# Who multiplies the high one-hots: ScalarE or GpSimd, in the routing stage of an attention and expert kernel

## The chip, the cores and the metric

The kernel runs on one core of one Trainium2 chip. The metric is the device time of one execution in microseconds (us). A core has five engines that run side by side and wait for one another by semaphores: TensorE (PE in the profile; its weight loads are PEld), VectorE (DVE), ScalarE (ACT), GpSimd (POOL) and SyncE (SP), which issues transfers.

## The reference, cut to what matters

The input x has 4096 rows of 256 numbers. It goes through a layer norm and cross attention, then through a layer norm and a block of 8 experts, of which each row takes two. The part that this case is about decides where each row goes:

```python
scores = softmax(x @ wg)                      # [4096, 8]
gates, idx = top_k(scores, 2)                 # two experts for each row
masks = one_hot(idx, 8)                       # [4096, 2, 8]
loc = cumsum(masks, 0) - 1 + offsets          # place in the expert's list
keep = loc_sel < C                            # C = 1280 places each
pos = where(keep, idx * C + loc_sel, E * C)
buf.at[pos].set(x)                            # rows sorted by expert
y = silu(disp @ fc1 + b1) @ fc2 + b2          # per expert
combined = sum(gates * ybuf[pos])             # back to the rows
```

The kernel needs the inverse of `pos`: for each of the 8 x 1280 = 10240 places, the number of the row that stands there. With that it gathers the rows of 256 places at a time.

## The kernel before, in words

**Stages.** For 32 tiles of 128 rows the attention runs until about 279 us of the profiled span. Then comes routing, the stage of this case. From about 309 us to 727 us the experts run: 40 steps of 256 places, each with transposes, a first and a second product on TensorE. A last stage adds and normalizes.

**The inverse table.** Each row's two choices give 64 columns of 128 choices (NC = 64, one per partition and column). A place number is split into `slot_hi` (which group of 128 places, 80 of them, NS = 80) and `slot_lo` (which of the 128). For each column two one-hot matrices are made:

- the low one, `oh_lo[:, n, :]`, 128 wide in bf16. Where the low number fits it holds the number of the row's tile plus one, elsewhere zero. VectorE makes it in one instruction a column (`lo_chunk`, L1478). ScalarE makes it in two (`lo_onehot`): a square of the difference into `apart` (L788), then a Relu that keeps what is zero (L793).
- the high one, `oh_id[:, ring, column, 1, :]`, 80 wide in bf16, made for a whole chunk of columns in one VectorE instruction (`hi_chunk`, L1474). A copy multiplied by the number of the partition, `oh_id[..., 0, :]`, stands beside it (`rows_of_chunk`, L802, on ScalarE before).

TensorE then multiplies: one matmul a column, 64 in all, added up in bank 2 (L1155, `placed` counts them). The half from `oh_id[..., 0, :]` gives row number times tile number, the half from `oh_id[..., 1, :]` gives the tile number. VectorE turns both into `slot_ids` (`rows_ids`, L1637 to L1651) and GpSimd gathers by them (L599).

**The order.** The code's order on each engine is the order in which it runs; nothing schedules it. The 64 columns are cut into chunks, and TensorE takes the chunks in the order of the table:

```python
CHUNKS = [(0, 7), (7, 14), (14, 21), (28, 37), (37, 46), (21, 28), (46, 55), (55, 64)]
BY_ACT = (0, 1, 2, 5)
RING = 5
```

Columns 0 to 27 (the early part) have their places before the last tiles are done. Columns 28 to 63 have theirs when VectorE has signalled `located` (after L1451). `BY_ACT` names the chunks whose low one-hots ScalarE makes; VectorE makes the others. `oh_id` is a ring of five chunks, so the sixth waits until TensorE has placed the first, and so on.

Beside this GpSimd makes the gates (L622 to L632). Behind its last product of the gates it waits for `ids_made` and starts the gathers. Behind its last low one-hot VectorE makes one low part of weights (`first_weights_lo(0)`, L1458), then waits for all 64 matmuls. Behind its last product ScalarE makes two high parts of weights (L729) and loads a table.

Of the kernel before, what the change touches and what calls it, by code (L numbers as in the profile page):

```python
# [5 lines left out]
def xattn_moe_kernel(nc, x, ctxT, wqT, bq, wkT, bk, wvT, bv, woT, wo, bo, boT, wg, w1T, b1T, w2, b2, gamma, beta, out):  # L6
# [13 lines left out]
    f32, f32r, bf16, i32 = mybir.dt.float32, mybir.dt.float32r, mybir.dt.bfloat16, mybir.dt.int32  # L20
    ALU, ACT, AX = mybir.AluOpType, mybir.ActivationFunctionType, mybir.AxisListType.X
    ds = bass.ds

    P = 128
# [38 lines left out]
    def wait(engine, sem, value):  # L63

        if not isinstance(value, int) or value > 0:
            engine.wait_ge(sem, value)
# [16 lines left out]
    with root:  # L83
        def sb(name, shape, dt=f32, where=root):
            return where.enter_context(nc.sbuf_tensor(name, shape, dt))
# [88 lines left out]
        hi_i = sb("hi_i", [P, NC], i32, A)  # L174
        slot_hi = sb("slot_hi", [P, NC], f32, A)
        slot_lo = sb("slot_lo", [P, NC], f32, A)
        CHUNKS = [(0, 7), (7, 14), (14, 21), (28, 37), (37, 46), (21, 28), (46, 55), (55, 64)]
        BY_ACT = (0, 1, 2, 5)
        RING = 5
        oh_lo = sb("oh_lo", [P, NC, P], bf16, A)  # L180
        oh_id = sb("oh_id", [P, RING, 9, 2, NS], bf16, A)
        apart = sb("apart", [P, 2, 7, P], bf16, A)
        sid = sb("sid", [P, NS], f32, A)
        tile_1 = sb("tile_1", [P, NS], f32, A)
# [66 lines left out]
        def sem(name):  # L251
            return sems[name]
# [71 lines left out]
        def columns_before(k):  # L324
            return sum(b - a for a, b in CHUNKS[:k])

# [112 lines left out]
        def _(pool):  # L439
# [163 lines left out]
            def scatter(st):  # L603

                if within(st, NST):
# [3 lines left out]
                    for q in range(2):  # L609
# [2 lines left out]
                                             y_sb[:, u, q, :], None, bounds_check=N + 4 * P - 1, oob_is_err=False,  # L612
                                             compute_op=ALU.add).then_inc(scattered[u], 16)

            pool.wait_ge(load_b1, 16)
            g.tensor_copy(b1_now[:, 0, :], b1_sb[:, 0:HJ]).then_inc(sem("b1_copied"), 1)

# [4 lines left out]
            g.tensor_tensor(e_all[:], below[:], rstd2[:].unsqueeze(2).to_broadcast([P, NT, NE]), ALU.mult)\  # L622
                .then_inc(sem("router_scaled"), 1)
            g.tensor_tensor(e_second[:], second[:], rstd2[:], ALU.mult).then_inc(sem("router_scaled"), 1)
            pool.wait_ge(sem("located"), 1)
            g.tensor_tensor(either[:], sel[:, 0], sel[:, 1], ALU.add).then_inc(sem("gate_parts"), 1)
            pool.wait_ge(sem("router_exp"), 2)
# [3 lines left out]
            pool.wait_ge(sem("gate_parts"), 2)  # L631
            g.tensor_tensor(gate_e[:], either[:], e_scale[:].unsqueeze(2).to_broadcast([P, NT, NE]), ALU.mult)\  # L632
                .then_inc(sem("gates_made"), 1)

            for u in range(2):
                pool.wait_ge(xn_stored[u], 32 * PAIRS)
# [30 lines left out]
        def _(act):  # L667
# [114 lines left out]
            def lo_onehot(k):  # L782

                a0, b0 = CHUNKS[k]
                i = BY_ACT.index(k)
                wait(act, sem("lo_made_act"), i - 1)
                for n in range(a0, b0):
                    m = a.activation(apart[:, i % 2, n - a0, :], iota_lo[:], ACT.Square, scale=-1.0,  # L788
                                     bias=slot_lo[:, n:n + 1])
                m.then_inc(sem("lo_apart"), 1)  # L790
                act.wait_ge(sem("lo_apart"), i + 1)
                for n in range(a0, b0):
                    m = a.activation(oh_lo[:, n, :], apart[:, i % 2, n - a0, :], ACT.Relu, scale=-float(n + 1),  # L793
                                     bias=tile_no[:, n:n + 1])
                m.then_inc(sem("lo_made_act"), 1)

            def rows_of_chunk(k):
                a0, b0 = CHUNKS[k]
                act.wait_ge(sem("hi_made"), k + 1)
                wait(act, sem("placed"), columns_before(k - RING + 1) if k >= RING else 0)  # L800
                o = oh_id[:, k % RING, 0:b0 - a0]
                a.activation(o[:, :, 0, :], o[:, :, 1, :], ACT.Copy, scale=my_row[:, 0:1]).then_inc(sem("row_made"), 1)  # L802

            act.wait_ge(sem("route_consts"), 10)
            act.wait_ge(sem("early_located"), 1)
# [2 lines left out]
            act.wait_ge(sem("router_scaled"), 2)  # L808
            a.activation(e_all[:], e_all[:], ACT.Exp).then_inc(sem("router_exp"), 1)
            a.activation(e_second[:], e_second[:], ACT.Exp).then_inc(sem("router_exp"), 1)  # L810
            rows_of_chunk(0)
            rows_of_chunk(1)
            lo_onehot(2)
            for k in (2, 3, 4):
                rows_of_chunk(k)
            lo_onehot(5)
            for k in range(5, len(CHUNKS)):
                rows_of_chunk(k)

            def rows_hi(gq, c):  # L820
                if within_st(gq, c):
# [439 lines left out]
        def _(dve):  # L1261
# [193 lines left out]
            def first_weights_lo(n):  # L1455
                dve.wait_ge(sem("w_hi_made"), n + 1)
                hi, lo, raw = w_parts(0, n)
                v.tensor_tensor(lo, raw, hi.bitcast(f32), ALU.subtract).then_inc(sem("w_lo_made"), 1)  # L1458
# [11 lines left out]
            def hi_chunk(k):  # L1470

                wait(dve, sem("placed"), columns_before(k - RING + 1) if k >= RING else 0)
                o, iota, at = hi_onehot(k)
                v.tensor_tensor(o, iota, at, ALU.is_equal).then_inc(sem("hi_made"), 1)  # L1474

            def lo_chunk(k):
                for n in range(*CHUNKS[k]):
                    m = v.tensor_scalar(oh_lo[:, n, :], iota_lo[:], slot_lo[:, n:n + 1], float(n % NT + 1),  # L1478
                                        ALU.is_equal, ALU.mult)
                m.then_inc(sem("lo_made"), 1)  # L1480
# [142 lines left out]
            lo_chunk(4)  # L1623
            hi_chunk(5)
            hi_chunk(6)
            lo_chunk(6)
            hi_chunk(7)
            lo_chunk(7)
            first_weights_lo(0)

            dve.wait_ge(sem("placed"), NC)
# [154 lines left out]
```

## Time and profile before

| what | value |
|---|---|
| median of 3 runs | 775.68 us (772.46 to 775.83) |
| the profiled execution, its own time | 773.96 us |
| its span in the trace | 772.2 us |
| busy over the span | PE 679.7 us, DVE 564.8, POOL 431.6, ACT 408.5 |
| routing, first low one-hot on ACT to last matmul of the table | 272.47 to 299.16 us |

The trace gives for each instruction its start from the span's beginning and its duration. Instructions that stand in one engine's queue without a wait overlap a little, so a duration can be longer than the distance from one start to the next; where an engine works through a row of them, the distance is what counts. Spans on POOL are rough.

### The profile page before, as it was taken

Reading aid. Unit: us, or ns where it says so; the run is one execution under the profiler, and the core shown is the slowest. Engines: PE = TensorE matmul, PEld = TensorE weight load, DVE = VectorE, ACT = ScalarE, POOL = GpSimd, SP = SyncE. Lnnn points to the kernel's source line nnn. Section 1 sums busy time; section 2 is a strip of 40 time slices with the busy share of each in tenths; the row PEclk is TensorE's granted clock in tenths of the full one; section 3 lists DMA queues with packets and bytes.
Section 4 is the critical chain, followed back from the end, with each engine's and each line's share of the span. In section 5 each row is a group of like instructions: output and inputs, shape, how many; then the busy total and the mean of one; then the engine's idle time right before and its main releaser. Section 6 shows DMA issues by size and latency. Waiting matters only on the chain.

```text
span 772.2 us, 15699 instructions
## 1 busy us (share of the span) xinstructions
PE 679.7 (88%) x5592; PEld 647.8 (84%) x5592; DVE 564.8 (73%) x1194; ACT 408.5 (53%) x963; POOL 431.6 (56%) x547
## 2 busy tenths in 40 slices
PE   5999999999999823999999999999999999999600
PEld 4789898888989723999999998999999999999500
DVE  5589898988887896666566669777596665854187
ACT  3445555555555585444544557455474454643185
POOL 6745565466465333535455558857577454632456
PEclk9789999999999955999999999999999999999855
DMA  9501011010110121533343456544455243322484
GB/s 295 173 15 42 30 41 41 31 42 29 42 40 31 42 84 39 174 81 55 88 105 45 101 111 119 118 81 94 102 116 115 46 103 57 58 28 29 55 273 149
DMA packets 55764, 64.10 MB, mean 83 GB/s; under 512 B 9472, under 2 KB 50944, under 8 KB 55552
## 3 DMA queue, kind: packets, MB, share of 16 engines
q0 software_dynamic: 15360, 21.31, 17.3%
q1 hardware_dynamic: 39616, 41.64, 16.5%
q8 instruction: 55, 0.90, 0.5%
q14 instruction: 29, 0.24, 0.1%
q10 hardware_dynamic: 704, 0.01, 0.0%
HBM read 39.22 MB, written 23.72 MB: 82 GB/s over the span
## 4 chain that ended last, share of the span: by engine, by line
PE 70%; DVE 19%; issue 4%; POOL 2%; ACT 2%; DMA 2%; POOLq 0%; SPq 0%; DVEq 0%; ACTq 0%
PE banks L898 18%; PE banks L900 17%; PE banks L899 17%; PE banks L1040 5%; PE banks L1026 3%; PE banks L1170 2%; DVE rowmax L1497 2%; PE banks L1014 2%; DVE vals L1465 2%; DVE xn1T_lo L1294 1%; DVE st L1271 1%; PE banks L1069 1%; DVE probs L1504 1%; PE banks L943 1%; DVE X L1556 1%
## 5 line engine op out<-in xcount | busy, mean ns | idle before, releaser
L611 POOL DMA_INDIRECT sum_rows<-y_sb,slot_ids x80 | 133.2, 1665 | 160.3 <-ACT y_sb L841 143.9
L851 ACT ACTIVATE hraw<-banks,b_now 128x256 f32<-128x256 f32 x320 | 132.3, 476 | 88.9 <-PE banks L900 81.5
L898 PE MATMUL banks<-xT_hi,w_hi 128*128 128x256 f32 x560 | 161.6, 289 | 1.7 <-ACT xT_hi L823 1.7
L900 PE MATMUL banks<-xT_hi,w_lo 128*128 128x256 f32 x560 | 158.5, 283 | 0.0
L899 PE MATMUL banks<-xT_lo,w_hi 128*128 128x256 f32 x560 | 158.4, 283 | 0.0
L898 PE MATMUL banks<-w_hi,h_hi 128*128 128x256 f32 x528 | 148.8, 282 | 1.3 <-issue 1.3
L899 PE MATMUL banks<-w_lo,h_hi 128*128 128x256 f32 x528 | 148.6, 281 | 0.0
L900 PE MATMUL banks<-w_hi,h_lo 128*128 128x256 f32 x528 | 148.5, 281 | 0.0
L1689 DVE TENSOR_TENSOR h_lo<-hraw,h_hi 128x512 fp32r<-128x512 f32 x160 | 113.8, 711 | 5.5
L1687 DVE CAST h_hi<-hraw 128x512 fp32r<-128x512 f32 x160 | 79.0, 494 | 44.8 <-ACT hraw L851 43.7
L898 PEld LDWEIGHTS banks<-xT_hi,w_hi 128*128 128x128 f32 x560 | 106.4, 190 | 2.2 <-issue 2.1
L599 POOL DMA_INDIRECT xg<-xn_rows,slot_ids x80 | 89.1, 1113 | 32.9 <-issue 32.3
L899 PEld LDWEIGHTS banks<-xT_lo,w_hi 128*128 128x128 f32 x560 | 106.5, 190 | 0.1
L900 PEld LDWEIGHTS banks<-xT_hi,w_lo 128*128 128x128 f32 x560 | 106.3, 190 | 0.0
L898 PEld LDWEIGHTS banks<-w_hi,h_hi 128*128 128x128 f32 x528 | 99.4, 188 | 1.7 <-issue 1.7
L738 ACT ACTIVATE probsT<-banks 124x384 f32<-124x384 f32 (+1 forms) x128 | 56.0, 437 | 84.5 <-PE banks L1026 84.3
L899 PEld LDWEIGHTS banks<-w_lo,h_hi 128*128 128x128 f32 x528 | 99.4, 188 | 0.0
L900 PEld LDWEIGHTS banks<-w_hi,h_lo 128*128 128x128 f32 x528 | 99.4, 188 | 0.0
L823 ACT ACTIVATE xT_hi<-banks 128x512 fp32r<-128x512 f32 x40 | 24.1, 602 | 115.2 <-PE banks L1170 107.2
L1040 PE MATMUL banks<-VB,probsT 124*128 124x51 f32 (+2 forms) x640 | 83.0, 268 | 0.0
L1040 PEld LDWEIGHTS banks<-VB,probsT 124*128 124x128 f32 x640 | 81.6, 192 | 0.0
L574 POOL TENSOR_TENSOR rstd<-var,minus_half 128x1 f32<-128x1 f32 x32 | 17.5, 547 | 98.3 <-DVE var L1575 98.3
(216 smaller groups left out, 1442.6 us busy)
## 6 DMA issues: line engine op xcount, KB each, us to landing
w1raw<-in_w1T SPq DMA_DIRECT2D x8, 1024.0 KB
w2raw<-in_w SPq DMA_DIRECT2D x8, 1024.0 KB
xn_rows<-xn SPq DMA_DIRECT2D x32, 128.0 KB, 1.8
sum_rows<-xn SPq DMA_DIRECT2D x32, 128.0 KB, 1.8
out<-z SPq DMA_DIRECT2D x16, 256.0 KB, 2.2
res<-sum_rows SPq DMA_DIRECT2D x7, 512.0 KB, 8.4
X<-in_x SPq DMA_DIRECT2D x2, 1280.0 KB, 12.4
xg<-xn_rows,slot_ids POOLq DMA_INDIRECT x80
```

The source lines that it names most:

```text
L599: g.indirect_dma_start(xg[:, st % XR, q, :], None, xn_rows, bass.IndirectOffsetOnAxis(ap=slot_ids[:, st, 0, q:q + 1], axis=0), bounds_chec ...
L611: g.indirect_dma_start(sum_rows, bass.IndirectOffsetOnAxis(ap=slot_ids[:, st, 1, q:q + 1], axis=0), y_sb[:, u, q, :], None, bounds_check=N ...
L738: a.activation(probsT[:, j0:j0 + w, :].rearrange("r j q -> r (j q)"), banks[0:JW, PT, 0:w * P], ACT.Copy).then_inc(sem("pT_made"), 1)
L823: a.activation(xT_hi[:, c % 2].rearrange("p c t -> p (c t)"), banks[:, XT, :], ACT.Copy)\
L851: a.activation(hraw[:, j // 2, j % 2, :], banks[:, j // 2, (j % 2) * 256:(j % 2 + 1) * 256], ACT.Silu, bias=b1_now[:, (c // SPE) % 2, j:j ...
L898: t_.matmul(o, a_hi, b_hi, start=first, stop=False)
L899: t_.matmul(o, a_hi, b_lo, start=False, stop=False)
L900: return t_.matmul(o, a_lo, b_hi, start=False, stop=last)
L1026: m = t_.transpose(banks[0:JW, PT, (j - j0) * P:(j - j0 + 1) * P], probs[:, 1 - u, f * KH + j * JS:f * KH + j * JS + JW], ident[:])
L1040: m = t_.matmul(banks[:, PV, f * VW + a_:f * VW + a_ + n_], probsT[:, NJ * f + j, :], VB[:, ds(((2 * b + f) * NJ + j) * VW + a_, n_)], sta ...
L1687: v.tensor_copy(hi, raw).then_inc(sem("h_hi_made"), 1)
L1689: v.tensor_tensor(lo, raw, hi.bitcast(f32), ALU.subtract).then_inc(sem("h_lo_made"), 1)
```

## The change

The multiplication of the high one-hots by the row number goes from ScalarE's `activation` with a scale to GpSimd's `tensor_scalar`. ScalarE gets one more chunk of low one-hots (chunk 6). There are nine chunks in place of eight: 7, 7, 7, 8, 8, 7, 7, 7 and 6 columns, where before there were four of 7 and four of 9. The ring's entries are 8 columns wide instead of 9. Since ScalarE now makes low one-hots for columns past 32 as well, its tile numbers are taken modulo NT = 32.

```diff
-        CHUNKS = [(0, 7), (7, 14), (14, 21), (28, 37), (37, 46), (21, 28), (46, 55), (55, 64)]
-        BY_ACT = (0, 1, 2, 5)
+        CHUNKS = [(0, 7), (7, 14), (14, 21), (28, 36), (36, 44), (21, 28), (44, 51), (51, 58), (58, 64)]
+        BY_ACT = (0, 1, 2, 5, 6)
         RING = 5
         oh_lo = sb("oh_lo", [P, NC, P], bf16, A)
-        oh_id = sb("oh_id", [P, RING, 9, 2, NS], bf16, A)
+        oh_id = sb("oh_id", [P, RING, 8, 2, NS], bf16, A)
...
+            def rows_of_chunk(k):
+                a0, b0 = CHUNKS[k]
+                pool.wait_ge(sem("hi_made"), k + 1)
+                wait(pool, sem("placed"), columns_before(k - RING + 1) if k >= RING else 0)
+                o = oh_id[:, k % RING, 0:b0 - a0]
+                g.tensor_scalar(o[:, :, 0, :], o[:, :, 1, :], my_row[:, 0:1], None, ALU.mult)\
+                    .then_inc(sem("row_made"), 1)
...
             g.tensor_tensor(e_second[:], second[:], rstd2[:], ALU.mult).then_inc(sem("router_scaled"), 1)
+            rows_of_chunk(0)
+            rows_of_chunk(1)
             pool.wait_ge(sem("located"), 1)
...
                 .then_inc(sem("gates_made"), 1)
+            for k in range(2, len(CHUNKS)):
+                rows_of_chunk(k)
...
-            def rows_of_chunk(k):
-                a0, b0 = CHUNKS[k]
-                act.wait_ge(sem("hi_made"), k + 1)
-                wait(act, sem("placed"), columns_before(k - RING + 1) if k >= RING else 0)
-                o = oh_id[:, k % RING, 0:b0 - a0]
-                a.activation(o[:, :, 0, :], o[:, :, 1, :], ACT.Copy, scale=my_row[:, 0:1]).then_inc(sem("row_made"), 1)
...
-            rows_of_chunk(0)
-            rows_of_chunk(1)
             lo_onehot(2)
-            for k in (2, 3, 4):
-                rows_of_chunk(k)
             lo_onehot(5)
-            for k in range(5, len(CHUNKS)):
-                rows_of_chunk(k)
+            act.wait_ge(sem("located"), 1)
+            lo_onehot(6)
...
             hi_chunk(6)
-            lo_chunk(6)
             hi_chunk(7)
             lo_chunk(7)
+            hi_chunk(8)
+            lo_chunk(8)
             first_weights_lo(0)
```

ScalarE's queue from the second exponential of the gates to the end of the table's work, before (`oh_id` with `my_row` is the multiplication, `apart` and `oh_lo` are the two halves of the low one-hots):

```order
L810 ACTIVATE e_second<-e_second 128x32
L802 ACTIVATE oh_id<-oh_id,my_row 128x7x80 [waits hi_made] x2
L788 ACTIVATE apart<-iota_lo,slot_lo 128x128 [waits lo_made_act]
L788 ACTIVATE apart<-iota_lo,slot_lo 128x128 x6
L793 ACTIVATE oh_lo<-apart,tile_no 128x128 [waits lo_apart]
L793 ACTIVATE oh_lo<-apart,tile_no 128x128 x6
L802 ACTIVATE oh_id<-oh_id,my_row 128x7x80 [waits hi_made]
L802 ACTIVATE oh_id<-oh_id,my_row 128x9x80 [waits hi_made] x2
```

and the last of it, in the changed kernel:

```order
L805 ACTIVATE oh_lo<-apart,tile_no 128x128 x6
L800 ACTIVATE apart<-iota_lo,slot_lo 128x128 [waits lo_made_act,located]
L800 ACTIVATE apart<-iota_lo,slot_lo 128x128 x6
L805 ACTIVATE oh_lo<-apart,tile_no 128x128 [waits lo_apart]
L805 ACTIVATE oh_lo<-apart,tile_no 128x128 x6
L741 ACTIVATE w_hi<-w2raw 128x1024 [waits load_w2] x2
```

All eight multiplications are gone from this queue, and a fifth set of 14 low one-hot instructions stands ahead of the weights.

GpSimd's queue from its second product for the gates to the first gather, before:

```order
L624 TENSOR_TENSOR e_second<-second,rstd 128x32
L626 TENSOR_TENSOR either<-sel 128x256 [waits located]
L629 TENSOR_TENSOR either<-either,e_all 128x256 [waits gate_parts,router_exp]
L632 TENSOR_TENSOR gate_e<-either,e_scale 128x256 [waits gate_parts,scale_made]
L599 DMA xg<-xn_rows,slot_ids 128x264 [waits gates_stored,ids_made,xn_stored1,xn_stored0]
```

and in the changed kernel:

```order
L632 TENSOR_TENSOR e_second<-second,rstd 128x32
L620 TENSOR_SCALAR oh_id<-oh_id,my_row 128x7x80 [waits hi_made] x2
L636 TENSOR_TENSOR either<-sel 128x256 [waits located]
L639 TENSOR_TENSOR either<-either,e_all 128x256 [waits gate_parts,router_exp]
L642 TENSOR_TENSOR gate_e<-either,e_scale 128x256 [waits gate_parts,scale_made]
L620 TENSOR_SCALAR oh_id<-oh_id,my_row 128x7x80 [waits hi_made]
L620 TENSOR_SCALAR oh_id<-oh_id,my_row 128x8x80 [waits hi_made] x2
L620 TENSOR_SCALAR oh_id<-oh_id,my_row 128x7x80 [waits placed,hi_made] x3
L620 TENSOR_SCALAR oh_id<-oh_id,my_row 128x6x80 [waits placed,hi_made]
```

Two multiplications stand between the products for the gates, seven behind them and ahead of the gathers.

VectorE's queue behind the scale of the gates, before:

```order
L1474 TENSOR_TENSOR oh_id<-iota_hi,slot_hi 128x7x80
L1474 TENSOR_TENSOR oh_id<-iota_hi,slot_hi 128x9x80
L1478 TENSOR_SCALAR oh_lo<-iota_lo,slot_lo 128x128 x9
L1474 TENSOR_TENSOR oh_id<-iota_hi,slot_hi 128x9x80
L1478 TENSOR_SCALAR oh_lo<-iota_lo,slot_lo 128x128 x9
L1474 TENSOR_TENSOR oh_id<-iota_hi,slot_hi 128x7x80 [waits placed]
L1474 TENSOR_TENSOR oh_id<-iota_hi,slot_hi 128x9x80 [waits placed]
L1478 TENSOR_SCALAR oh_lo<-iota_lo,slot_lo 128x128 x9
L1474 TENSOR_TENSOR oh_id<-iota_hi,slot_hi 128x9x80 [waits placed]
L1478 TENSOR_SCALAR oh_lo<-iota_lo,slot_lo 128x128 x9
L1458 TENSOR_TENSOR w_lo<-w1raw,w_hi 128x1024 [waits w_hi_made]
```

and in the changed kernel:

```order
L1475 TENSOR_TENSOR oh_id<-iota_hi,slot_hi 128x7x80
L1475 TENSOR_TENSOR oh_id<-iota_hi,slot_hi 128x8x80
L1479 TENSOR_SCALAR oh_lo<-iota_lo,slot_lo 128x128 x8
L1475 TENSOR_TENSOR oh_id<-iota_hi,slot_hi 128x8x80
L1479 TENSOR_SCALAR oh_lo<-iota_lo,slot_lo 128x128 x8
L1475 TENSOR_TENSOR oh_id<-iota_hi,slot_hi 128x7x80 [waits placed] x3
L1479 TENSOR_SCALAR oh_lo<-iota_lo,slot_lo 128x128 x7
L1475 TENSOR_TENSOR oh_id<-iota_hi,slot_hi 128x6x80 [waits placed]
L1479 TENSOR_SCALAR oh_lo<-iota_lo,slot_lo 128x128 x6
L1459 TENSOR_TENSOR w_lo<-w1raw,w_hi 128x1024 [waits w_hi_made]
```

VectorE makes 29 low one-hots here where it made 36, and seven sets of high ones where it made six.

## Rows read from the trace of the kernel before

**Rows 1.** Chain of waits, 290 to 299 us: start, length, engine, tile, line.

```profile
290.04 0.90 ACT oh_id L802
290.94 2.05 ACT apart L788 x7
...
293.32 1.84 ACT oh_lo L793 x6
295.17 0.66 ACT oh_id L802
...
295.96 3.20 PE banks L1155 x25
```

**Rows 2.** Stretches, located to last matmul: busy PE, PEld, DVE, ACT, POOL; PEclk; DMA.

```profile
284.70:299.20 14.50, 7.04 (x50) 5.95 (x50) 13.10 (x46) 12.82 (x30) 2.81 (x3) 0.52 0.14 11
```

**Rows 3.** Timeline, TensorE in the same stretch: start, length, line, operation.

```profile
287.79 1.09 PE L1155 MATMUL banks<-oh_id,oh_lo 128*128 128x160 bf16 x7 [3.51 <-ACT oh_id L802]
...
295.96 3.19 PE L1155 MATMUL banks<-oh_id,oh_lo 128*128 128x160 bf16 x25 [3.05 <-ACT oh_id L802]
```

**Rows 4.** Timeline, VectorE with GpSimd idle, and VectorE behind the table.

```profile
289.11 0.90 DVE L1474 TENSOR_TENSOR oh_id<-iota_hi,slot_hi 128x720 bf16<-128x720 bf16 x1
289.93 1.54 DVE L1478 TENSOR_SCALAR oh_lo<-iota_lo,slot_lo 128x128 bf16<-128x128 bf16 x9
291.39 1.55 DVE L1474 TENSOR_TENSOR oh_id<-iota_hi,slot_hi 128x560 bf16<-128x560 bf16 x2
292.87 1.54 DVE L1478 TENSOR_SCALAR oh_lo<-iota_lo,slot_lo 128x128 bf16<-128x128 bf16 x9
...
296.61 1.21 DVE L1458 TENSOR_TENSOR w_lo<-w1raw,w_hi 128x1024 fp32r<-128x1024 f32 x1
...
299.19 0.17 DVE L1637 TENSOR_SCALAR tile<-banks 128x10 f32<-128x10 f32 x1 [1.36 <-PE banks L1155]
```

**Rows 5.** Timeline, VectorE and GpSimd side by side, two places.

```profile
278.96 0.64 POOL L622 TENSOR_TENSOR e_all<-below,rstd 128x256 f32<-128x256 f32 x1 [4.34 <-DVE sel L1403]
279.03 1.17 DVE L1474 TENSOR_TENSOR oh_id<-iota_hi,slot_hi 128x560 bf16<-128x560 bf16 x1
279.57 0.75 POOL L624 TENSOR_TENSOR e_second<-second,rstd 128x32 f32<-128x32 f32 x1
...
285.93 1.42 DVE L1474 TENSOR_TENSOR oh_id<-iota_hi,slot_hi 128x720 bf16<-128x720 bf16 x1
286.73 1.11 POOL L632 TENSOR_TENSOR gate_e<-either,e_scale 128x256 f32<-128x256 f32 x1
...
287.28 0.61 DVE L1478 TENSOR_SCALAR oh_lo<-iota_lo,slot_lo 128x128 bf16<-128x128 bf16 x1
```

**Rows 6.** Groups, GpSimd: line, operation, shapes, count | busy us, mean ns.

```profile
L450 POOL TENSOR_SCALAR_AFFINE_SELECT key_of_row<-key_of_row 77x616 f32<-77x616 f32 x1 | 0.8, 773 | 0.0
L442 POOL MEMSET key_of_row<- 77x616 f32 x1 | 0.6, 612 | 0.0
L466 POOL MEMSET zero_row<- 128x256 f32 x1 | 0.3, 302 | 0.0
L447 POOL TENSOR_SCALAR_AFFINE_SELECT ident<-ident 128x128 f32<-128x128 f32 x1 | 0.3, 287 | 0.2 <-POOL head_of_row L444 0.2
```

**Rows 7.** Line L486: durations in ns, least, median, most.

```profile
L486 POOL TENSOR_TENSOR KH_lo<-kT_lo,head_of_feature x8: 1217/1223/1714, 11.7 to 25.0; 128x616 fp32r<-128x616 f32 x8
```

**Rows 8.** Timeline, ScalarE from the gates' second exponential.

```profile
281.25 0.21 ACT L810 ACTIVATE e_second<-e_second 128x32 f32<-128x32 f32 x1
...
282.67 2.14 ACT L788 ACTIVATE apart<-iota_lo,slot_lo 128x128 bf16<-128x128 bf16 x7
...
286.90 1.53 ACT L802 ACTIVATE oh_id<-oh_id,my_row 128x560 bf16<-128x560 bf16 x2
```

**Rows 9.** Timeline, VectorE's steps to the places of the late columns.

```profile
281.61 0.17 DVE L1428 CAST tokens_e<-scan_e 128x8 int32<-128x8 f32 x1
...
282.37 0.46 DVE L1435 TENSOR_TENSOR place<-place,sel 128x288 f32<-128x288 f32 x1
```

More of the change, by code:

```diff
@@ L792, in lo_onehot @@
                 for n in range(a0, b0):
-                    m = a.activation(oh_lo[:, n, :], apart[:, i % 2, n - a0, :], ACT.Relu, scale=-float(n + 1),
-                                     bias=tile_no[:, n:n + 1])
+                    m = a.activation(oh_lo[:, n, :], apart[:, i % 2, n - a0, :], ACT.Relu, scale=-float(n % NT + 1),
+                                     bias=tile_no[:, n % NT:n % NT + 1])
                 m.then_inc(sem("lo_made_act"), 1)
-            def rows_of_chunk(k):
-                a0, b0 = CHUNKS[k]
-                act.wait_ge(sem("hi_made"), k + 1)
-                wait(act, sem("placed"), columns_before(k - RING + 1) if k >= RING else 0)
-                o = oh_id[:, k % RING, 0:b0 - a0]
-                a.activation(o[:, :, 0, :], o[:, :, 1, :], ACT.Copy, scale=my_row[:, 0:1]).then_inc(sem("row_made"), 1)
             act.wait_ge(sem("route_consts"), 10)
```

## The prediction, made before the changed kernel ran

> **What bounds the kernel now.** I read the page's chain first, to see which stage the change is in and whether that stage is on the path to the end. It is: between the attention and the experts TensorE has nothing to do but the 64 matmuls of the table, and the gathers can't start without it. So each microsecond of this stage is one of the kernel, and nothing outside the stage is touched.
>
> Then the chain of waits inside the stage. Its last part [rows 1] runs through ScalarE: the multiplication of chunk 4 (290.04), the low one-hots of chunk 5 (290.94 to 295.17), the multiplication of chunk 5, and only then 25 matmuls in one go (295.96 to 299.16). The reader is to see that the bound is ScalarE's queue. Chunk 5 is an early chunk, its columns are known long before, but ScalarE comes to it late, and chunks 6 and 7 pile up behind it on TensorE. TensorE's timeline [rows 3] says the same: 3.05 us idle before these 25, released by ScalarE's `oh_id`.
>
> Last the busy times of the stage [rows 2]: of 14.50 us VectorE is busy 13.10, ScalarE 12.82, GpSimd 2.81. ScalarE is the bound, but VectorE is only a step behind: its last low one-hots are done at 296.61 [rows 4], 2.6 us before the last matmul. GpSimd looks free. Whether it is free is what decides this case.
>
> **ScalarE's part.** Removed are eight multiplications; those of chunks 0 and 1 stand between 281.46 (end of the exponentials) and 282.67, and the low one-hots of a chunk of 7 take 282.67 to 286.90 = 4.23 us [rows 8]. The new queue is three such sets back to back: 281.46 + 3 x 4.23 = 294.15 for the end of chunk 6. If nothing else bounded, TensorE would take the seven matmuls of chunk 6 in 1.09 us [rows 3] and could be through with chunk 8 soon behind. So ScalarE's bound moves about 2.5 us forward, from which the gain would come. The new wait for `located` sits before the third set, at 289.9, when `located` (284.7) is long past; behind it in ScalarE's queue stand only two high parts of weights, which come earlier than before. It costs nothing.
>
> **VectorE's own work.** From rows without GpSimd beside them [rows 4]: nine low one-hots take 289.93 to 291.39 = 1.46 us, 0.162 each; a high set of 9 columns 289.11 to 289.93 = 0.82; one of 7 and one of 9 together 291.39 to 292.87 = 1.48, so 0.66 for 7, 0.08 a column, hence 0.74 for 8 and 0.58 for 6. From 285.93 on, where the second late high set starts [rows 5], before: high 0.66 + 4 x 0.82 = 3.94, low 36 x 0.162 = 5.83, together 9.77. After: high 3 x 0.66 + 2 x 0.74 + 0.58 = 4.04, low 29 x 0.162 = 4.70, together 8.74. VectorE saves 1.03 us. The actual stretch before was 296.61 - 285.93 = 10.68, so 0.91 us of it was something else.
>
> **What that 0.91 us was: GpSimd.** Rows 5 show it at two places. At 278.96 GpSimd starts `e_all` and ends at 279.60. The high set that VectorE issues at 279.03 lasts 1.17 us instead of 0.66 to 0.75 and ends at 280.20, about 0.6 behind GpSimd's end. GpSimd's next, on 32 elements, lasts 0.75 us and ends at 280.32, right behind VectorE's end. The second place is `located`: the set of 9 columns takes 1.42 us instead of 0.90, GpSimd's `gate_e` then takes 1.11, ending 0.49 behind VectorE's end (287.35), and the first low one-hot takes 0.61 instead of 0.24, ending at 287.89, 0.05 behind `gate_e` (287.84). The two engines take turns: each waits for the other's instruction to end. Both VectorE kinds that matter here (the high sets with two SBUF inputs, the bf16 low one-hots) are held. About 0.15 us of an instruction's start is hidden in the wait (`e_all` alone 0.64, `gate_e` behind a wait 0.49).
>
> The Trainium skill, "SBUF — State Buffer", in its part on the physically separate sides, states the rule: the port pair that VectorE and GpSimd share is an exclusive lock, held for the full instruction, taken by VectorE's two-port modes and by its instructions with two SBUF inputs. By that rule the trace agrees at both places (1.42 against 0.90 us), and the rule speaks against this change: by it every multiplication on GpSimd is time that VectorE stands still, where on ScalarE it held nobody up.
>
> **What the multiplications cost on GpSimd.** No row shows GpSimd's `tensor_scalar`, so I bound it. Seven chunks (2 to 8), 50 columns of 80 = 4000 elements a partition, fall behind 284.7. Low end: a memset, which reads nothing: (612 - 302) / (616 - 256) = 0.86 ns an element [rows 6]. Nearest kind, one tensor in and one out: the affine selects, (773 - 287) / (616 - 128) = 1.00 ns [rows 6]. High end, two inputs: (1217 - 640) / (616 - 256) = 1.60 ns, from L486 [rows 7] and `e_all` [rows 5]. To this comes the start that the wait doesn't hide: `gate_e` 0.49 us against 256 x 1.60 = 0.41, so some 0.07 us each, 0.5 for seven. Together 3.9, 4.5 or 6.9 us. I take 4.5, since the operation reads one tensor and a scalar for each partition. Below nothing it can't be, as VectorE does the rest of its work anyway.
>
> The Trainium skill, "GPSIMD Engine Reference", section 3.1, gives about 1.8 cycles an element as the best case of a tight loop, at 1.2 GHz. The estimate by that figure is 1.5 ns an element, 6.0 + 0.5 us in all, and the sum below would be +4.3.
>
> Can VectorE use the time in which GpSimd holds the pair? No: its queue between 285.93 and the end is nothing but instructions of the kinds that are held, and it has no wait of its own there. GpSimd gets its turn quickly, too: it queues its request and gets in at the next boundary, as `gate_e` did between the high set and the first low one-hot. So the multiplications of chunks 2 and 3 go in between the first low one-hots of chunk 3, and each later one right behind its high set. That of chunk 8 lies ahead of VectorE's last six low one-hots, so all seven are on the path.
>
> **The sum.** VectorE ends its one-hots at 296.61 - 1.03 + 4.5 = 300.08. The last six matmuls wait for its last instruction (another 0.08): 300.15, a handoff of 0.05, and 0.97 for six (1.09 less one step of (3.19 - 1.09) / 18 = 0.117) [rows 3] give 301.2, against 299.16. TensorE becomes dependent on VectorE in place of ScalarE. VectorE's `w_lo` (1.21 us [rows 4]) was hidden in the wait for the matmuls with 1.4 us to spare; now it runs 300.08 to 301.29 and ends just behind the matmuls, so the next step starts at 301.3 against 299.19: +2.1.
>
> The first two multiplications run in the earlier part, behind the second high set (280.20 plus its 0.7, so 280.9), to about 282.2 at 1.00 ns. TensorE's first chunks wait for them no longer than before. VectorE has there a cast at 281.61 and a product with two SBUF inputs at 282.37 [rows 9]; either can be caught for part of a multiplication, between nothing and 0.6 us. I take 0.2. The other steps there read PSUM or are tiny. Only one thing more is moved past on GpSimd: the gates' sum of the two selections waits for `located` at 284.7, over 2 us behind the second multiplication, and the store of the gates goes out as before, since seven of nine multiplications come behind it. The gathers wait for `ids_made`, when GpSimd has been done for over a microsecond.
>
> In all +2.1 + 0.2 = +2.3 us. From there the stage's successors run as before, only later. Against the profiled execution's own 773.96 that is 776.3. That execution is 1.7 us under the median of the three runs; the mean of all four times is 774.5. I predict 774.5 + 2.3 = 776.8. By the low price the sum is +1.5 (less 0.6, less the 0.2); by the high one +2.3 + 2.4 + 0.4 = +5.1, that is 779.6.
>
> **Rivals.**
>
> Overlap: the multiplication with one tensor input holds VectorE up little. Then VectorE ends at 285.93 + 8.74 + 0.91 = 295.58 and ScalarE's 294.15 is ahead of it. The last six matmuls end at 296.6 and `w_lo` at 296.8, so the next step starts 2.4 us earlier: 772.1. For it speaks that all contests in rows 5 are with GpSimd instructions of two tensor inputs. Against it: what was held there was held to the end of the instruction, not in proportion. This is the case with the other sign. It decides from the point where the seven multiplications take less than 2.3 us of VectorE's time.
>
> A dear multiplication: GpSimd needs 1.4 ns an element or more, in bf16 with a gap of 80 between the columns and a scalar from memory. Rows 7 stand for it; that the affine selects, which read one tensor, run at 1.00 stands against it. From 6.1 us for the seven on, the loss is over 3.9 us. Typical: +5.1, 779.6. VectorE would still be the engine waited for, and GpSimd busy half of the stage.
>
> Something behind the stage: gathers, weight loads and TensorE's clock meet otherwise when shifted. TensorE is granted 0.52 of full speed in the stage [rows 2], about the lower of its two levels, and it runs at that level whichever way the table is made. The four times before, over 3.4 us apart, bound what such a shift is worth: some 1.7 us either way.
>
> **How the numbers follow.** Forecast, taking turns at 0.86 to 1.4 ns: 0.60. Dear: 0.20. Overlap: 0.14. Something else: 0.06. What a measurement can tell from no change is about 0.5%, 3.9 us. The forecast is inside it but for the spread of the runs (0.05 slower), the dear case is outside with 0.15 of its 0.20, overlap falls mostly inside (faster by over 0.5% with 0.05), and something else gives 0.02 each way. Faster 0.07, same 0.71, slower 0.22. The range reaches from the overlap case, less a little, to the high end of the price: 771.7 to 780.3.
>
> **What would show it.** In the trace after: nine `oh_id` instructions on GpSimd of 0.6 to 0.9 us alone and longer behind VectorE; VectorE's one-hots stretched wherever one stands beside them, three of the low ones of chunk 3 among them, and the stretch from the second late high set to `w_lo` about 14 us instead of 10.7; ScalarE through with chunk 6 at about 294; TensorE's last gap released by VectorE's `oh_lo`, and only six matmuls behind it. The last matmul at about 301. I am wrong if VectorE's low one-hots run at 0.16 us beside GpSimd, or if a multiplication lasts over 1.1 us by itself.

## The result: 0.45% slower, and GpSimd is the engine that TensorE waits for

The changed kernel took 778.84 us (median of 14 runs, 775.06 to 781.12) against 774.67 us before (14 runs, 771.06 to 780.67). The ratio is 1.0045, 95% interval 1.0027 to 1.0062: by the ratio 2.1 to 4.8 us, about 3.5, slower. The profiled execution has a span of 776.6 us, 4.4 more than before.

The stage shows nearly all of it. I count it from the start of the first high set to the end of the last matmul of the table, since what comes ahead of it shifts by up to 3 us from run to run. Before: 279.03 to 299.15 [rows 3, 5] = 20.12 us. After: 279.39 to 303.28 = 23.89 us, so 3.8 more.

Some tenths of that are TensorE's clock. Before, TensorE was granted 0.50 (1.2 GHz, the lower of its two levels) through the last 25 matmuls until 298.7 us, and 1.0 (2.4 GHz, the higher) for the last 0.45 us of them. The changed kernel's last matmuls ran at 0.50 to the end. One of the probe runs below has the same stage as the kernel before: there the 25 ran at 0.50 throughout, took 3.49 instead of 3.19 us, and the stage took 20.42. VectorE's part repeats: the end of its last low one-hot, from the first high set, is at 17.65 to 17.66 us in all three traces of this stage.

TensorE in the changed kernel, from the third chunk on (start, length, line, operation, in brackets the idle time and what ended it):

```profile
290.46 1.09 PE L1156 MATMUL banks<-oh_id,oh_lo 128*128 128x160 bf16 x7 [4.48 <-POOL oh_id L620]
...
292.83 1.23 PE L1156 MATMUL banks<-oh_id,oh_lo 128*128 128x160 bf16 x8 [1.27 <-POOL oh_id L620]
...
294.69 1.22 PE L1156 MATMUL banks<-oh_id,oh_lo 128*128 128x160 bf16 x8 [0.64 <-POOL oh_id L620]
...
297.15 1.09 PE L1156 MATMUL banks<-oh_id,oh_lo 128*128 128x160 bf16 x7 [1.24 <-POOL oh_id L620]
...
298.82 1.09 PE L1156 MATMUL banks<-oh_id,oh_lo 128*128 128x160 bf16 x7 [0.57 <-POOL oh_id L620]
...
300.59 1.09 PE L1156 MATMUL banks<-oh_id,oh_lo 128*128 128x160 bf16 x7 [0.69 <-POOL oh_id L620]
...
302.33 0.95 PE L1156 MATMUL banks<-oh_id,oh_lo 128*128 128x160 bf16 x6 [0.64 <-POOL oh_id L620]
```

The 25 matmuls in one go of [rows 3] are gone. Chunk follows chunk, and each waits for the same thing: GpSimd's multiplication. The other three engines in the same stretch:

```profile
281.73 2.14 ACT L800 ACTIVATE apart<-iota_lo,slot_lo 128x128 bf16<-128x128 bf16 x7
...
286.73 1.34 DVE L1475 TENSOR_TENSOR oh_id<-iota_hi,slot_hi 128x640 bf16<-128x640 bf16 x1
...
287.99 2.41 DVE L1479 TENSOR_SCALAR oh_lo<-iota_lo,slot_lo 128x128 bf16<-128x128 bf16 x8
...
288.54 13.65 POOL L620 TENSOR_SCALAR oh_id<-oh_id,my_row 128x560 bf16<-128x560 bf16 x7
...
290.79 2.71 DVE L1479 TENSOR_SCALAR oh_lo<-iota_lo,slot_lo 128x128 bf16<-128x128 bf16 x8
292.36 2.15 ACT L805 ACTIVATE oh_lo<-apart,tile_no 128x128 bf16<-128x128 bf16 x7
...
299.62 1.21 DVE L1459 TENSOR_TENSOR w_lo<-w1raw,w_hi 128x1024 fp32r<-128x1024 f32 x1
...
303.32 0.17 DVE L1639 TENSOR_SCALAR tile<-banks 128x10 f32<-128x10 f32 x1 [2.49 <-PE banks L1156]
```

To be seen are three ends. ScalarE is through with its five sets at 294.5. VectorE is through with its one-hots at 299.62 and then, after its part of the weights, idle for 2.49 us; before it was 1.36 [rows 4]. GpSimd works at its last seven multiplications without a pause from 288.54 to 302.19, 1.95 us each, and TensorE's last six matmuls start 0.14 us later. The busy times of the stretch have changed places against [rows 2] (PE, PEld, DVE, ACT, POOL in the order of the columns):

```profile
285.40:303.30 17.90, 8.34 (x55) 5.99 (x52) 15.36 (x40) 12.42 (x35) 16.36 (x10) 0.50 0.11 9
```

GpSimd is now the busiest, 16.36 of 17.90 us. One line says why (durations in ns, least, median, most):

```profile
L620 POOL TENSOR_SCALAR oh_id<-oh_id,my_row x9: 1680/1879/2485, 280.7 to 300.4; 128x560 bf16<-128x560 bf16 x6, 128x640 bf16<-128x640 bf16 x2, 128x480 bf16<-128x480 bf16 x1
```

I had put a multiplication of 560 elements at 0.6 to 0.9 us. It takes 1.68 at least.

### The profile page after: what moved, and what is told of

It reads as the page before. It is cut to its first block, busy times and chain, and to the rows that moved or that the text cites. A ratio compares the mean times of both kernels' runs of the same rounds, so it can differ in the third digit from the quotient of the medians.

```text
span 776.6 us, 15711 instructions
## 1 busy us (share of the span) xinstructions
PE 681.1 (88%) x5592; PEld 647.6 (83%) x5592; DVE 568.2 (73%) x1188; ACT 406.6 (52%) x969; POOL 448.4 (58%) x556
## 4 chain that ended last, share of the span: by engine, by line
PE 70%; DVE 17%; issue 6%; ACT 4%; DMA 2%; POOL 1%; POOLq 0%; SPq 0%; DVEq 0%; ACTq 0%
PE banks L899 18%; PE banks L900 17%; PE banks L901 17%; PE banks L1041 5%; PE banks L1027 3%; DVE rowmax L1498 2%; PE banks L1171 2%; PE banks L1015 2%; DVE vals L1466 1%; ACT oh_lo L805 1%; ACT apart L800 1%; DVE st L1272 1%; DVE xn1T_lo L1295 1%; PE banks L1070 1%; DVE probs L1505 1%
```

## The experiments

Two theories stood after this. Pace (theory 1): a multiplication costs GpSimd 1.7 us by itself, seven come in a row, and TensorE follows. Turns (theory 2): the multiplications are cheap, but VectorE and GpSimd stand in each other's way, and VectorE is the bound (the forecast). From the first results came a third. Hold (theory 3): a part of each multiplication shuts VectorE out, and which of both engines binds depends on the form. "Hold" is below the time that one instruction of GpSimd takes from VectorE.

The table gives the stage in all versions, in us from the start of the first high set, each from one profiled execution; the ratio is to the kernel before, over all runs, with its 95% interval:

| version | VectorE's last low one-hot ends | last matmul ends | ratio of times |
|---|---|---|---|
| before | 17.66 | 20.12 | 1 |
| changed | 20.31 | 23.89 | 1.0045 (1.0027 to 1.0062) |
| chunk 6's low one-hots back on VectorE | 22.14 | 23.19 | 1.0069 (1.0048 to 1.0090) |
| multiplication back on ScalarE | 16.59 | 24.24 | 1.0064 (1.0040 to 1.0087) |
| multiplication on VectorE | 19.52 | 20.17 | 1.0010 (0.9990 to 1.0030) |
| GpSimd, as a tensor_tensor | 23.57 | 24.61 | 1.0083 (1.0050 to 1.0117) |
| three columns on GpSimd, the rest on VectorE | 20.30 | 21.34 | 1.0012 (0.9988 to 1.0037) |
| balanced | 18.58 | 19.62 | 0.9987 (0.9966 to 1.0009) |

**The price by itself.** A tail of probes, that is instructions for measuring alone, behind the last addition of the kernel before:

```diff
+            for _ in range(3):
+                probe(g.tensor_scalar(o7()[0], o7()[1], pr_n[:, 0:1], None, ALU.mult))
...
+            for _ in range(3):
+                probe(g.tensor_tensor(o7()[0], o7()[1], pr_n[:, 0:1].unsqueeze(2).to_broadcast([P, 7, NS]), ALU.mult))
+            for _ in range(3):
+                probe(g.tensor_copy(o7()[0], o7()[1]))
```

> The kernel before, with a tail of probes behind its last addition; its outputs are as before and its time is longer by the tail. GpSimd multiplies with nothing beside it, three times each: the changed kernel's form (bf16, 7 columns of 80 with a gap of 80, scalar from memory), the same with one column, bf16 without a gap, f32 without a gap, with a constant as the scalar, as a tensor_tensor with the row number broadcast, and a plain copy. Then VectorE makes 32 low one-hots beside four multiplications, and again beside four of the tensor_tensor form. Theory 1 (GpSimd's own pace: the multiplication costs 1.7 to 1.9 us by itself, some 3 ns an element): 1.6 to 1.8 us alone, and about 0.3 to 0.4 us with one column. Theory 2 (it costs 0.75 us as forecast and is stretched by VectorE's turns): 0.7 to 0.9 us alone and 1.7 only beside VectorE. For the hold: theory 1 has VectorE lose about 0.5 us for each multiplication, four of 32 low one-hots at over 0.5 us, 32 in about 5.2 + 2 us; if the port were held for the whole instruction, VectorE would lose 1.7 us each. The tensor_tensor form, two inputs, should hold it for its whole length, 1 us or more.

Measured, with no other engine at work (least, median, most in ns; L685 the form of the changed kernel, L687 one column, L690 bf16 without gaps, L692 f32 without gaps, L694 a constant as the scalar, L696 the tensor_tensor, L698 the copy):

```profile
L685 POOL TENSOR_SCALAR pr_bf<-pr_bf,pr_n x3: 1684/1684/1697, 774.6 to 778.2; 128x560 bf16<-128x560 bf16 x3
L687 POOL TENSOR_SCALAR pr_bf<-pr_bf,pr_n x3: 484/484/485, 780.0 to 781.1; 128x80 bf16<-128x80 bf16 x3
L690 POOL TENSOR_SCALAR pr_bf<-pr_bf,pr_n x3: 1684/1684/1685, 781.7 to 785.3; 128x560 bf16<-128x560 bf16 x3
L692 POOL TENSOR_SCALAR pr_f<-pr_f,pr_n x3: 1684/1685/1685, 787.0 to 790.6; 128x560 f32<-128x560 f32 x3
L694 POOL TENSOR_SCALAR pr_bf<-pr_bf x3: 1609/1609/1610, 792.4 to 795.7; 128x560 bf16<-128x560 bf16 x3
L696 POOL TENSOR_TENSOR pr_bf<-pr_bf,pr_n x3: 1120/1121/1121, 797.4 to 799.8; 128x560 bf16<-128x560 bf16 x3
L698 POOL COPY pr_bf<-pr_bf x3: 649/655/657, 801.0 to 802.4; 128x560 bf16<-128x560 bf16 x3
```

The price is the operation's own: (1684 - 484) / 480 = 2.50 ns an element and 0.28 us to start. Neither the dtype nor the gap makes it, and a constant as the scalar only 0.08 us of it. The pace theory's number for seven columns is right; for one column it had 0.3 to 0.4 us, and 0.48 were measured. What I did not expect is the order: the same product as a tensor_tensor with two inputs costs a third less, a copy 0.65 us. In the same run 32 low one-hots on VectorE took 7.68 us beside four of the multiplications and 8.75 beside four tensor_tensors. The second probe below has both again, with the time without GpSimd.

**Less to do for GpSimd.**

```diff
-                o = oh_id[:, k % RING, 0:b0 - a0]
+                o = oh_id[:, k % RING, 0:3]
                 g.tensor_scalar(o[:, :, 0, :], o[:, :, 1, :], my_row[:, 0:1], None, ALU.mult)\
...
+            def rest_of_rows(k):
+                a0, b0 = CHUNKS[k]
+                dve.wait_ge(sem("hi_made"), k + 1)
+                o = oh_id[:, k % RING, 3:b0 - a0]
+                v.tensor_scalar(o[:, :, 0, :], o[:, :, 1, :], my_row[:, 0:1], None, ALU.mult)\
+                    .then_inc(sem("rest_made"), 1)
...
```

Each `rest_of_rows` stands in VectorE's queue behind its high set, and TensorE waits for both parts of a chunk.

> The changed kernel, but GpSimd multiplies only three columns of each chunk (0.284 + 240 x 0.0025 = 0.88 us by the probe) and VectorE the other three to five (0.25 us each). GpSimd's pace is then out of the way. If GpSimd's hold on VectorE is a fixed 0.5 to 0.6 us for an instruction whatever its length, VectorE ends at 7.3 + 0.5 + 8.7 + 0.9 + 7 x 0.8 = 23.0 and the stage takes 24 us; if it is in proportion to length (a third), VectorE ends at 7.3 + 0.5 + 8.7 + 0.9 + 7 x 0.5 = 20.9 and the stage takes 21.9.

The stage took 21.34 us, 2.6 less than the changed kernel's, and VectorE ended at 20.30, where it had ended at 20.31. The bound has passed to VectorE, whose `oh_lo` releases the last matmuls:

```profile
300.90 0.98 PE L1157 MATMUL banks<-oh_id,oh_lo 128*128 128x160 bf16 x6 [0.90 <-DVE oh_lo L1487]
```

So it was GpSimd's pace that cost the changed kernel these 2.6 us. The other 1.2 against before, of which 0.3 can be the clock, came with VectorE as the bound. Both sub-theories of the hold expected too much, the proportional one less so (21.9): with a multiplication on VectorE of some 0.3 us, VectorE's end leaves about 0.1 us of hold for each of these short instructions.

**VectorE with more work.**

```diff
-        BY_ACT = (0, 1, 2, 5, 6)
+        BY_ACT = (0, 1, 2, 5)
...
             hi_chunk(6)
+            lo_chunk(6)
             hi_chunk(7)
```

> The changed kernel, but chunk 6's seven low one-hots go back to VectorE. Theory 1 (TensorE follows GpSimd's multiplications, one each 1.7 to 1.9 us, and VectorE has some 2.5 us to spare): the last matmul as in the changed kernel, about 303.3 within 0.4, time within 0.5 us of the changed kernel's. Theory 2 (VectorE, robbed by GpSimd, is the bound): VectorE's seven more cost 1.1 us, and the last matmul comes at 304.4 with VectorE's oh_lo as its releaser.

23.19 us: not the 25.0 that VectorE as the bound would have made, but 0.7 less than the changed kernel, which neither theory said. VectorE's end moved by 1.8 us to 22.14, and GpSimd's was 22.09, where it had been 22.79. Both engines now end together and VectorE releases the last two chunks:

```profile
301.21 1.09 PE L1154 MATMUL banks<-oh_id,oh_lo 128*128 128x160 bf16 x7 [0.65 <-DVE oh_lo L1477]
...
302.95 0.96 PE L1154 MATMUL banks<-oh_id,oh_lo 128*128 128x160 bf16 x6 [0.65 <-DVE oh_lo L1477]
```

GpSimd gained at two places. The high sets of chunks 5 to 7 no longer follow one another, and the multiplication that had run beside them took 1.83 us instead of 2.48. The last one, which had run beside VectorE's `w_lo`, took 1.50 us instead of 1.76. It lost 0.24 us of this by waiting for VectorE's last high set. That the neighbours on VectorE are the cause is argued from these rows and not tested by itself. The total times don't show the 0.7 us: the ratio is even the higher of the two, and the intervals overlap.

**The other part of the change alone.** Nine chunks and five sets on ScalarE, the multiplications there too (GpSimd's `rows_of_chunk` as `a.activation` on ScalarE, as before):

> The changed kernel's nine chunks and ScalarE's five sets of low one-hots, but the multiplications stay on ScalarE: the other part of the change alone. ScalarE's queue is 281.5 + 3 x 4.23 + 9 multiplications of 0.66 to 0.82 = about 300.8, and the last six matmuls follow in 1 us: last matmul at 301.7 to 302.3, ScalarE its releaser, 2.5 to 3 us slower than before (ratio 1.003 to 1.004), about a microsecond better than the changed kernel. If VectorE or GpSimd bound the changed kernel by anything else than the multiplications, this would be no better than it.

24.24 us, 4.1 more than before where 2.5 to 3 were expected, and not a microsecond better than the changed kernel but 0.3 worse:

```profile
291.34 0.83 ACT L802 ACTIVATE oh_id<-oh_id,my_row 128x640 bf16<-128x640 bf16 x1 [1.34 <-DVE oh_id L1477]
...
302.07 2.83 PE L1158 MATMUL banks<-oh_id,oh_lo 128*128 128x160 bf16 x20 [3.79 <-ACT oh_id L802]
```

The releaser is ScalarE as expected, but its queue stood 1.34 us waiting for VectorE's high set of chunk 4 before it could go on to chunk 5's low one-hots, and behind ScalarE's last sets 20 matmuls had piled up on TensorE, not six. With this order of the queues a fifth set on ScalarE pays only if the multiplications leave it. This version also shows VectorE's part without any multiplication beside it: from the second late high set to `w_lo` it took 287.55 to 297.16 = 9.61 us.

**The multiplication on VectorE.**

```diff
+            def rows_on_dve(k):
...
+                    a0, b0 = CHUNKS[k]
+                    dve.wait_ge(sem("hi_made"), k + 1)
+                    o = oh_id[:, k % RING, 0:b0 - a0]
+                    v.tensor_scalar(o[:, :, 0, :], o[:, :, 1, :], my_row[:, 0:1], None, ALU.mult)\
+                        .then_inc(sem("row_made"), 1)
...
```

> The changed kernel, but VectorE multiplies the high one-hots itself, right behind the high sets; GpSimd does none. Theory 1 with the estimate that VectorE takes 0.2 to 0.3 us for one (four elements a cycle at best, a little over its 0.16 us for a low one-hot): seven late ones add 1.4 to 2.1 us to VectorE in place of 3.3 us that GpSimd takes from it, the first two 0.5 us ahead of the late places; VectorE ends its one-hots at about 297.3, the last matmul is at about 298.5, some 0.5 to 1 us earlier than in the kernel before and 4 to 5 us earlier than in the changed one. Ratio to before 0.998 to 1.000. Rival (a bf16 multiplication with gaps runs at one element a cycle, 0.65 us each): 4.6 us for the late seven, the last matmul at 302, no better than the changed kernel by more than 1 us.

20.17 us, 3.7 less than with GpSimd, and no gain over before: expected was 0.5 to 1 us of it. Part of the miss is the expectation's own sum: its terms give 299.62 - 3.3 + 1.4 to 2.1 + 0.5 = 298.2 to 298.9 for VectorE's end, not 297.3. And the 20.17 are helped by the clock: the last six matmuls took 0.59 us at a granted clock of 1.0 (2.4 GHz), where they take 0.98 at 0.50 (1.2 GHz) in the balanced version. VectorE's timeline:

```profile
296.82 0.66 DVE L1471 TENSOR_SCALAR oh_id<-oh_id,my_row 128x560 bf16<-128x560 bf16 x2
297.40 0.72 DVE L1463 TENSOR_TENSOR oh_id<-iota_hi,slot_hi 128x560 bf16<-128x560 bf16 x1
298.16 0.39 DVE L1471 TENSOR_SCALAR oh_id<-oh_id,my_row 128x560 bf16<-128x560 bf16 x1
298.46 1.22 DVE L1476 TENSOR_SCALAR oh_lo<-iota_lo,slot_lo 128x128 bf16<-128x128 bf16 x7
```

Two multiplications cost 0.58 us (296.82 to 297.40), 0.29 each, 0.30 and the wait for the set before it where one stands alone. Over the same stretch in three versions, from the second late high set to `w_lo`, VectorE took 9.61 us without multiplications, 11.96 with its own seven (289.55 to 301.51) and 12.89 beside GpSimd's seven (286.73 to 299.62): 0.34 us each when it makes them itself, 0.47 when GpSimd does. VectorE does the work in less time than it loses by giving it away.

**The cheaper form on GpSimd.**

```diff
-                g.tensor_scalar(o[:, :, 0, :], o[:, :, 1, :], my_row[:, 0:1], None, ALU.mult)\
+                g.tensor_tensor(o[:, :, 0, :], o[:, :, 1, :],
+                                my_row[:, 0:1].unsqueeze(2).to_broadcast([P, b0 - a0, NS]), ALU.mult)\
```

> The changed kernel with GpSimd's multiplication written as a tensor_tensor with the row number broadcast, which took 1.12 us in the probe instead of 1.68, but from which 32 low one-hots on VectorE lost 0.87 us each instead of 0.6. The stage is counted from the start of the first high set to the end of the last matmul: 20.12 us before, 23.89 in the changed kernel. Theory 1, the pace of GpSimd's multiplications alone: with VectorE losing 0.5 each as now, VectorE ends at 7.3 + 8.7 + 0.9 + 3.5 = 20.5 from the first high set, stage 21.5. Theory 3, the longer hold decides once GpSimd is quicker: VectorE ends at 7.3 + 8.7 + 0.9 + 7 x 0.87 = 23.0, stage 24 us, no better than the changed kernel, and TensorE's last waits are for VectorE's oh_lo.

24.61 us: the hold theory's side (24), not the pace theory's (21.5), and 0.7 more than the changed kernel, though the instruction is a third shorter. The intervals of the two ratios overlap, so the times don't tell the two kernels apart. TensorE's end:

```profile
300.68 1.12 PE L1157 MATMUL banks<-oh_id,oh_lo 128*128 128x160 bf16 x7 [0.60 <-DVE oh_lo L1480]
303.03 0.98 PE L1157 MATMUL banks<-oh_id,oh_lo 128*128 128x160 bf16 x6 [1.23 <-DVE oh_lo L1480]
```

This is the kernel that my forecast described: GpSimd ahead (it stands 1.35 us idle before its last multiplication), VectorE robbed and the bound.

**The hold by itself.** Again a tail of probes, 32 low one-hots or eight high sets on VectorE beside GpSimd's instructions:

> The kernel before with another tail of probes; its outputs are as before and its time is longer by the tail. 32 low one-hots on VectorE, first alone, then beside GpSimd's multiplication of seven columns (four times), of three (six times), of one (eight times), and its tensor_tensor form (four times); then eight high sets of seven columns on VectorE, alone, beside the multiplication of seven, of three, and beside the tensor_tensor form. If a multiplication takes from VectorE a part in proportion to its length (0.6 of 1.8 us in the first probe, a third), 32 low one-hots take 5.2 us alone, 7.6 beside four of seven columns, 7.0 beside six of three, 6.4 beside eight of one. If it is a fixed 0.5 to 0.6 us each: 7.6, 8.5 and 9.5. The high sets: alone 5.3 us for eight; by the changed kernel, where none of them was stretched beside a tensor_scalar, 5.3 beside the multiplications too, while GpSimd's instruction gets longer (2.4 instead of 1.8); beside the tensor_tensor form 9 us.

VectorE (32 low ones alone, beside four multiplications of 7 columns, six of 3, eight of 1, four tensor_tensors; then eight high sets alone, beside multiplications of 7, of 3, beside tensor_tensors):

```profile
776.78 5.29 DVE L1775 TENSOR_SCALAR pr_lo<-iota_lo,pr_n 128x128 bf16<-128x128 bf16 x32 [4.93 <-POOL pr_f L695]
782.26 7.68 DVE L1775 TENSOR_SCALAR pr_lo<-iota_lo,pr_n 128x128 bf16<-128x128 bf16 x32 [0.19 <-POOL pr_f L695]
790.20 6.65 DVE L1775 TENSOR_SCALAR pr_lo<-iota_lo,pr_n 128x128 bf16<-128x128 bf16 x32 [0.25 <-POOL pr_f L695]
797.10 5.35 DVE L1775 TENSOR_SCALAR pr_lo<-iota_lo,pr_n 128x128 bf16<-128x128 bf16 x32 [0.25 <-POOL pr_f L695]
802.71 8.75 DVE L1775 TENSOR_SCALAR pr_lo<-iota_lo,pr_n 128x128 bf16<-128x128 bf16 x32 [0.25 <-POOL pr_f L695]
811.71 5.30 DVE L1778 TENSOR_TENSOR pr_hi<-iota_hi,pr_f 128x560 bf16<-128x560 bf16 x8 [0.25 <-POOL pr_f L695]
817.20 6.66 DVE L1778 TENSOR_TENSOR pr_hi<-iota_hi,pr_f 128x560 bf16<-128x560 bf16 x8 [0.19 <-POOL pr_f L695]
826.19 5.86 DVE L1778 TENSOR_TENSOR pr_hi<-iota_hi,pr_f 128x560 bf16<-128x560 bf16 x8 [2.33 <-POOL pr_f L695]
835.00 8.97 DVE L1778 TENSOR_TENSOR pr_hi<-iota_hi,pr_f 128x560 bf16<-128x560 bf16 x8 [2.95 <-POOL pr_f L695]
```

A multiplication of seven columns takes (7.68 - 5.29) / 4 = 0.60 us of VectorE's time, of three 0.23 (in the version with three columns it was about 0.1), of one 0.01; a tensor_tensor 0.87. So it is neither fixed nor the whole instruction, and for short ones less than in proportion. The 7.68 and the 8.75 us are those of the first probe again. High sets are held here too, 1.36 us over the multiplications that fell beside them, against the expectation. In the changed kernel they were not: three in a row took 2.03 us there as in the version with the multiplication on ScalarE, and GpSimd's instruction beside them took 2.48 instead of 1.68. Why the probe and the kernel differ in this stays open. What in the instruction holds the port, and why a tensor_scalar leaves it free for two thirds of its time, no run here shows.

**A version from what was learned.** From the one with all on VectorE, chunks 7 and 8 multiplied by ScalarE, which has time behind its last set:

```diff
+        CHUNKS = [(0, 7), (7, 14), (14, 21), (28, 36), (36, 44), (21, 28), (44, 52), (52, 58), (58, 64)]
...
+            for k in (7, 8):
+                a0, b0 = CHUNKS[k]
+                act.wait_ge(sem("hi_made"), k + 1)
+                act.wait_ge(sem("placed"), columns_before(k - RING + 1))
+                o = oh_id[:, k % RING, 0:b0 - a0]
+                a.activation(o[:, :, 0, :], o[:, :, 1, :], ACT.Copy, scale=my_row[:, 0:1]).then_inc(sem("row_made"), 1)
...
-            first_weights_lo(0)
...
             rows_ids(0, SPE)
+            first_weights_lo(0)
             first_weights_lo(1)
```

> A version meant to beat both: VectorE multiplies chunks 0 to 6, ScalarE 7 and 8 behind its low one-hots, where it was idle; chunks of 7, 7, 7, 8, 8, 7, 8, 6, 6 columns, of which ScalarE makes the low one-hots of the sixth, of the 8 behind it and of the first three; VectorE's first low part of the weights moves behind the first slot ids. From the version with all multiplications on VectorE (stage 20.17) this takes one low one-hot and two multiplications off VectorE, 0.16 + 0.7: stage 19.3 us against 20.12 before, and the step behind the table starts 19.4 us from the first high set against 20.16. Time 0.7 us under the kernel before, ratio 0.999, too little for the times to tell; rival: ScalarE comes late with the last two multiplications and the stage stays at 20.1.

19.62 us, half a microsecond under the kernel before and 4.3 under the changed one; expected was 19.3. VectorE's end came 0.94 us earlier than in the version with all multiplications on VectorE, against 0.86 expected; the missing 0.3 us are the clock again, since here the last six matmuls took 0.98 us at a granted clock of 0.50 and there 0.59 at 1.0. The ratio to before, 0.9987 (0.9966 to 1.0009), is not told from no change. Against the changed kernel it is better: the intervals of the two ratios don't touch.

## Why the prediction came out, and which of its steps did not

Forecast was +2.3 us and 776.8 us, measured +3.5 (2.1 to 4.8) and 778.84: same side, within the range, in the band of 0.5%. But the mechanism behind it was wrong, and the time came out by two errors of opposite sign, which is luck. By the start of the step behind the table, counted from the first high set, the sum is: +2.3 forecast, less 1.0 because VectorE was held less than I had it, plus 2.5 because TensorE waited for GpSimd beyond VectorE's end, +3.8 in all (23.93 against 20.15 us).

The prediction's own sign of being wrong came: a multiplication lasts over 1.1 us by itself, 1.68. The step that failed is the price of GpSimd's multiplication, and with it the claim that VectorE is the engine waited for.

- **ScalarE's part** held. It was through at 294.5 in the changed kernel (forecast 294.15, in an execution that reached the stage 0.36 us later), and the wait for `located` cost nothing.
- **VectorE's own work** held: 1.03 us less was forecast, and the version with the multiplication on ScalarE shows 9.61 us for the stretch that took 10.68 before.
- **The price failed.** 0.86 to 1.60 ns an element were my ends; it is 2.50, and 0.28 us to start, where I had 0.07. The seven multiplications were 4.5 us in the sum, 6.9 at the most; they took 13.65. I ordered GpSimd's operations by how many tensors they read, and put the multiplication beside the affine selects [rows 6] with the two-input L486 [rows 7] as the ceiling. The probe shows that the order is not that. The "dear" rival was right that GpSimd needs over 1.4 ns, but its loss of over 3.9 us came from VectorE being held all that time, and it kept VectorE as the engine waited for.
- **The hold failed.** I read rows 5 rightly for the tensor_tensors there (the probe: 0.87 of 1.12 us) and gave it to an operation that the trace didn't have. From the second late high set to `w_lo` VectorE took 286.73 to 299.62 = 12.89 us, of which 8.74 its own and 0.91 the gates. The remaining 3.24 are 0.46 for each of seven multiplications of 1.95 us on average, not all of it (0.47 by the version with 9.61 us). The stretch was to be about 14 us. The other rival, overlap, was right that most of a multiplication runs beside VectorE's work, but had the time 2.4 us shorter than before, with the wrong sign.
- **The bound failed with them.** I had VectorE end at 300.08 + 0.2 and TensorE wait for it. VectorE ended at 299.62, in an execution 0.36 us later, so 1.0 us earlier than forecast, but TensorE waited for GpSimd, whose own queue I had only costed as a burden on VectorE: "GpSimd gets its turn quickly, too" was as far as I looked. 0.46 instead of 0.64 us a piece saved VectorE 1.3 us (of which the first two multiplications took back 0.2), and seven multiplications in a row cost TensorE 2.5 us beyond VectorE's end.
- **The first two multiplications** took 2.17 and 1.90 us (forecast 0.65) and ran over the steps to `located`. One step there was held, `hi_i` at 0.62 instead of 0.18 us; `located` came 0.43 us later from the first high set, where I had taken 0.2.
- **`w_lo`** stayed hidden, since TensorE was later than VectorE. With the multiplication on VectorE it was exposed: the next step stood 0.40 us behind the last matmul, 20.57 us from the first high set, 0.4 later than before.

## What to carry to other kernels

An engine that looks free costs twice: its own time for the operation in just this form, which no neighbour in the trace gives, and what it takes from the engine whose port it shares. Measure both before moving work, by a probe with the exact operation alone and beside the other engine's. Here VectorE spends 0.34 us on a multiplication that costs it 0.47 us when GpSimd does it, so this work belonged on VectorE rather than on GpSimd. And add up the receiving engine's queue as a bound of its own, not only as a disturbance of the one that you believe to be the bound.

## What the runs showed of the hardware

- GpSimd's `tensor_scalar`: 0.28 us and 2.50 ns an element a partition, from instructions of 80 and 560 elements with nothing beside them, the same for bf16 and f32, with gaps and without; 1.61 us instead of 1.68 for 560 elements with a constant. As a tensor_tensor with a broadcast second input 1.12 us for 560 elements, a copy 0.65.
- The Trainium skill, "SBUF — State Buffer", in its part on the physically separate sides, has the loser of the shared port fully blocked for the whole instruction. For the tensor_tensor the runs come near it (0.87 of 1.12 us). For the tensor_scalar they don't: 32 low one-hots on VectorE lost 0.60 us to each of 1.87 us, and 0.01 to each of those with one column, which take 0.48 us alone. The measurement decides.
- VectorE makes the same product of 560 bf16 elements in 0.29 us.
